# GpSimd applies both layer norms, between its products with C, in a state-space and mixture-of-experts layer

## The reference, cut to what matters

```python
def _layernorm(x, axis=-1, eps=1e-05):
    m = jnp.mean(x, axis=axis, keepdims=True)
    v = jnp.var(x, axis=axis, keepdims=True)
    return (x - m) / jnp.sqrt(v + eps)

h = _L0_tok_ref(x)
h = h + _L0_attn_ref(_layernorm(h, axis=-1), ...)   # y = sum over n of h[n] * C[n], h by a scan
h = h + _L0_ffn_ref(_layernorm(h, axis=-1), ...)
```

## Time and profile before

| | us |
|---|---|
| median of 3 runs | 3821.16 (3820.72 to 3831.04) |
| profiled execution, its own time | 3815.21 |
| span of the trace | 3813.3 |
| busy PE / DVE / ACT / POOL | 3190.2 / 3016.4 / 2879.0 / 2106.1 |
| share of the span PE / DVE / ACT / POOL | 84% / 79% / 75% / 55% |

### The profile page before, as it was taken

How to read it: one execution, slowest core, us unless ns; L and a number is a source line. 1 busy time by engine, 2 the same in 40 slices (tenths; PEclk the granted TensorE clock), 3 DMA queues, 4 the chain that set the end, 5 groups by cost and what they waited for, 6 DMA issues and landing times. The chain is left out here.

```text
span 3813.3 us, 65702 instructions
## 1 busy us (share of the span) xinstructions
PE 3190.2 (84%) x19681; PEld 2528.9 (66%) x19681; DVE 3016.4 (79%) x5267; ACT 2879.0 (75%) x5580; POOL 2106.1 (55%) x780
## 2 busy tenths in 40 slices
PE   5898898988888888888888898898898888566664
PEld 3777776776777677777777777676677667445453
DVE  3888888888888888888888888888888898544442
ACT  4998988888888888888888888888888888121110
POOL 0555555555555555555555555555555556157776
PEclk8999999999999999999999999999999998678887
DMA  2111111111111111111111111111111111157775
GB/s 84 47 47 55 55 43 56 57 57 55 51 53 40 56 57 57 57 57 52 54 57 57 57 55 43 57 57 57 49 56 52 40 52 50 42 135 146 147 151 86
DMA packets 175733, 241.57 MB, mean 63 GB/s; under 512 B 32816, under 2 KB 154128, under 8 KB 175376
## 3 DMA queue, kind: packets, MB, share of 16 engines
q1 hardware_dynamic: 150800, 199.44, 16.3%
q0 software_dynamic: 24576, 37.77, 6.0%
HBM read 176.07 MB, written 61.08 MB: 62 GB/s over the span
## 5 line engine op out<-in xcount | busy, mean ns | idle before, releaser
L345 POOL TENSOR_TENSOR hid<-hid,c_all 128x1536 f32<-128x1536 f32 x512 | 1771.0, 3459 | 1491.6 <-DVEq L563 1489.6
L568 DVE TENSOR_TENSOR_SCAN hid<-decay,hid,psB 128x512 f32<-128x512 f32 x1024 | 1310.7, 1280 | 119.3 <-PE psB L826 12.4
L826 PE MATMUL psB<-ident,dbu_t 128*128 128x128 f32 x6144 | 936.7, 285 | 236.8 <-DVE hid L568 224.0
L363 ACT ACTIVATE dbu_t<-dtu_t,b_t 128x512 f32<-128x512 f32 x1536 | 995.5, 714 | 159.8 <-PE psB L826 158.2
L375 ACT ACTIVATE decay<-dt,a_neg 128x383 f32<-128x383 f32 x2048 | 1085.8, 606 | 0.0
L826 PEld LDWEIGHTS psB<-ident,dbu_t 128*128 128x128 f32 x6144 | 721.8, 145 | 446.6 <-DVE hid L568 325.7
L838 PE MATMUL psY<-ident,hid 128*128 128x128 f32 x6144 | 780.7, 278 | 33.1 <-POOL hid L345 32.3
L838 PEld LDWEIGHTS psY<-ident,hid 128*128 128x128 f32 x6144 | 714.2, 145 | 77.6 <-POOL hid L345 34.4
L568 DVE TENSOR_TENSOR_SCAN hid<-decay,psB 128x512 f32<-128x512 f32 x512 | 624.0, 1219 | 103.4 <-PE psB L826 72.0
L898 PE MATMUL psM<-u,w_dt 128*128 128x384 f32 x1024 | 354.7, 489 | 18.3 <-ACT turned L384 14.7
L898 PEld LDWEIGHTS psM<-u,w_dt 128*128 128x128 f32 x1024 | 184.4, 190 | 127.8 <-ACT turned L384 21.3
(11 more groups left out here) (148 smaller groups left out, 3520.4 us busy)
## 6 DMA issues: line engine op xcount, KB each, us to landing
c_all<-bc_rows_dram SPq DMA_DIRECT2D x128, 768.0 KB, 4.9
out_dram<-h SPq DMA_DIRECT2D x64, 384.0 KB, 3.5
h<-out_dram SPq DMA_DIRECT2D x32, 384.0 KB, 3.4
x_weights_dram<-normed SPq DMA_DIRECT2D x32, 384.0 KB, 2.5
xs<-in_x_dram SPq DMA_DIRECT2D x32, 256.0 KB
e_wg<-in_gate_dram SPq DMA_DIRECT2D x64, 128.0 KB
e_wu<-in_up_dram SPq DMA_DIRECT2D x64, 128.0 KB
e_wd<-in_down_dram SPq DMA_DIRECT2D x64, 128.0 KB
```

What stands on the lines that cost most here:

```text
L345: nc.gpsimd.tensor_tensor(hid[k % 4][:, :, :], hid[k % 4][:, :, :], c_all[:, k, :].unsqueeze(1).to_broadcast([P, CH, L]), ALU.mult).then_i ...
L363: last = nc.scalar.activation(dbu_t[k % 2][:, t, :], dtu_t[q][:, t, :], ACT.Copy, scale=b_t[q][:, t, k:k + 1])
L568: nc.vector.tensor_tensor_scan(h[:, lo:hi], flat(decay[k % 4])[:, lo:hi], psB[:, j, :], h[:, lo - 1:lo] if j else 0.0, ALU.mult, ALU.add). ...
L826: last = nc.tensor.transpose(psB[:, j, i * P:(i + 1) * P], dbu_t[k % 2][:, t, c * P:(c + 1) * P], ident[:, :])
```

## The change

Three pieces. `norm` on DVE keeps the four small operations (as `full_rstd`) and loses the three that apply the norm, together with their waits. POOL gets them, between its products: the second norm ahead of product 4, the first ahead of product 13. POOL's loop of 32 bodies becomes the list of `each`. DVE gets two new waits, for POOL to be done with `h1` before `attended` overwrites it and with `mv[1]` before `second_stats` does.

```diff
-            with pool.Fori(0, NB) as b:
+            def norm(n, j, src, to):
+
+                pool.wait_ge(s_rs[j], n + 1)
+                if j == 1:
+                    pool.wait_ge(s_xst, 16 * (n + 1))
+                pool.sem_inc(s_turn, 1)
+                for s in range(NSEG):
+                    last = nc.gpsimd.tensor_scalar(to[:, s, :], src[:, s, :], mv[j][:, s, 0:1],
+                                                   rstd[j][:, s:s + 1], ALU.subtract, ALU.mult)
+                last.then_inc(s_xn[j], 1)
+
+            def body(b, q, scans, back, late, routed, front, early):
                 for k in range(NS):
-                    times_c(b, k)
+                    if late and k == 4:
+                        norm(b - 2, 1, h2, normed2)
+                    if early and k == 13:
+                        norm(b + 2, 0, h1, normed1)
+                    if scans:
+                        times_c(b, k)
+
+            each(pool, body)
...
-            def norm(n, j, src, to):
+            def full_rstd(n, j):
...
                 nc.vector.tensor_tensor(rstd[j][:, :], t[:, 2, :], y, ALU.mult).then_inc(s_rs[j], 1)
-                dve.wait_ge(s_rs[j], n + 1)
-                if j == 1:
-                    dve.wait_ge(s_xst, 16 * (n + 1))
-                for s in range(NSEG):
-                    last = nc.vector.tensor_scalar(to[:, s, :], src[:, s, :], mv[j][:, s, 0:1],
-                                                   rstd[j][:, s:s + 1], ALU.subtract, ALU.mult)
-                last.then_inc(s_xn[j], 1)
...
                 after(dve, s_h1st, 16 * a)
+                after(dve, s_xn[0], a)
...
             def second_stats(o, b):
+                after(dve, s_xn[1], o)
...
                         if k == 5:
-                            norm(o, 1, h2, normed2)
+                            full_rstd(o, 1)
...
                         if k == 14:
-                            norm(a, 0, h1, normed1)
+                            full_rstd(a, 0)
```

## The result

The changed kernel takes 3863.9 us (median of 4 runs, 3862.47 to 3868.53) beside 3820.94 (4 runs, 3817.2 to 3831.04) for the kernel before: a ratio of 1.0118 with a 95% interval of 1.0102 to 1.0134. It is 43 us slower, not 19 faster. The profiled execution has a span of 3860.3 us, 47 more than before.

What follows compares the result with a forecast made beforehand. No engine was full; waits between PE, DVE and ACT bound the kernel, DVE leading in steps 10 to 5. 20.8 - 2 = 19 us off 3815.2 gave 3796 profiled, so 3802 median; forecast's own range 3795 to 3811, overall 3782 to 3819.

Steps and rivals of the forecast that it cites:

- What leaves DVE: Before the scans of steps 14 and 5: without the norm's three operations the scan begins 0.84 us earlier.
- Step 14: First norm, beside scans in 30 bodies: 0.84 us gained in 17, 0.5 in 13 at loop turns, entry or exit; 20.8 us.
- PE's wait of step 2: PE's 2.14 us wait in step 2 stays about as long, since PE and DVE both move.
- the loop turn: Where the two-body loop turns, PE leads and holds scan 0, so step 14 gains only 0.5 us.
- T: POOL's time for a norm's three operations: 1.5 us, 0.5 each, bounds 1.0 to 10.4; PE waits for products from 3.1.
- rival C: At products 4 and 13, POOL's operation is dear: at 2 us each, 99 us lost, 3920 us; chance 0.08.
- Beside whom it runs: Product 4 overhanging into step 6 could hold L723, DVE's first two-input operation: 0.2 us at T = 1.8, costed at nothing.
- DVE's 3.4 us of waits: DVE's three waits for PE and ACT in step 10, said to grow from 2.5 to 3.4 us.
- the prediction's own signs of being wrong: PE waiting for products, L723 or L725 stretched to over 1 us, or waits in step 10 as long as before.
- rival A: Step 5 pays too, as step 10's waits shrink: 25 us more, 3777 us; chance 0.10.
- the ends: Where the pipeline fills and drains, serial chains take T plus a handover instead of 1.06 us: 4 x 0.5 = 2 us lost.
- Step 5's gain: Second norm, 30 times 0.84 us off DVE, costed at nothing since step 10's waits grow; 25 us if that cover isn't real.

Runs made afterwards that it cites:

- e2: Changed kernel with the second norm applied on DVE again and only the first on POOL; ratio 0.9987 to the kernel before.
- e1: Kernel before with only POOL's program changed, from a loop of 32 one-body turns to the list with a two-body loop; ratio 0.9995 to the kernel before.
- e4: Changed kernel, both norms on POOL, with POOL's program as a loop of one-body turns; ratio 1.0131 to the kernel before.
- e5: Changed kernel with POOL applying the second norm to one of three parts only, the rest left zero; ratio 0.9991 to the kernel before.
- e10: Changed kernel with `route_experts` moved on DVE from step 6 to step 8, nothing left out; ratio 1.0013 to the kernel before.
- e7: Changed kernel with 67 empty instructions at the start of DVE's program; ratio 1.0095 to the kernel before.

## Why the prediction was wrong

**Right.** What leaves DVE: 0.76 us for each norm instead of 0.84, since the gap before the scan is 0.26 behind the refinement and not 0.17. Step 14: the gain is real (13 to 14 shorter by 0.76, shortest sum of e2 lower by 0.63, 16 us in 26 bodies beside 20.8 for 30), and PE follows it. PE's wait of step 2 stays. At the loop turn the gain isn't the smaller 0.5 us of the prediction: the interval from scan 13 to 14 is shorter by 0.76 there too, and e2's turn is no later than before (29.6 us beside 31.0)., from which the prediction read that PE leads at a turn, is of a turn at which PE's granted clock was 0.50 (1671.65 to 1674.47 us of the kernel before); over its twelve loop turns the gap before scan 0 goes from 0.20 to 0.86 us. PE hardly waits for products (at most 0.6 us, once in two sequences; the prediction had such waits begin at T = 3.1). POOL's turned loop costs nothing (e1, e4), and in the waits of the steady stretch DVE doesn't wait for POOL once, so its two new waits cost nothing either. The operation that a product can hold was named correctly.

**The size that was off: POOL's operation.** The prediction took 0.5 us from an AFFINE_SELECT and the product's rate; it takes 1.22, and T is 3.62 us, not 1.5. That is 4.8 ns a column against the product's 2.25. The rows it was taken from are of operations with one step per element and no scalar from a tile; this form has two of each, which may be why, though no run varied it. T stayed inside the bounds (1.0 to 10.4), but what was made of the far side was only rival C at 0.08. The Trainium skill (GPSIMD Engine Reference, Engine selection) calls one-input operations on GpSimd roughly line-rate; here it took 3.4 times DVE's 1.06 us. The prediction's estimate of 2.1 us used that section's figure for two inputs, and was low too.

**The step that failed.** It is in "Beside whom it runs": a hold of L723 would lie "inside DVE's 3.4 us of waits. Nothing." The place was right, and so was the arithmetic: with 0.2 us at T = 1.8 the same line gives 3.62 - 1.6 = 2.0 us at the T measured, and 1.9 came. The price was wrong. The waits it was charged to lie in step 10, and PE needs scan 6 and 7 long before. In step 6 PE has no slack for a late scan (0.35 and 0.74 us of waits at once), so the delay goes on to PE and ACT, the work of PE that DVE awaits in step 10 is late by the same amount, and the waits there stay 0.51, 1.03 and 0.99. Slack of this kind takes up DVE being earlier (part of the second norm's gain, by e5), not DVE being later: a wait for somebody who is himself delayed doesn't shrink. Two of the prediction's own signs of being wrong came with it: L723 (now L736) over 1 us, and waits in step 10 as long as before, which it would have read as rival A. In the bodies 4 to 29 the hold costs 26 x 1.9 = 49 us, and the kernels in which it is gone took 48 (e5) and 40 us (e10) less than the changed kernel.

Rival C named POOL's dear operation, with the break-even at T = 4 to 4.7 from PE's need of the products. Those points held: at 3.62 PE waits hardly at all. The loss came through the other consumer of POOL's time, the shared access to SBUF, whose threshold was at T = 1.6. Its price was not weighed against a T beyond 1.8, though the range of T went to 10.4.

**Not foreseen.** The late instructions: 24 of the 47 us in the profile. Some 15 of them are halts of DVE at the loop turn and in step 1; e7 shows that they follow the program's places. The other 9 are step 9, PE's clock, and this difference may be chance, since kernels with the DVE program of before spread from 5.3 to 12.5 us. The prediction counted DVE's removed instructions as time won and gave no thought to the program's places moving. And the ends: 4 x 0.5 us was taken and 11 came. The bodies there pay the block too, and the norm that costs 3.62 stands in serial chains. Step 5's gain, costed at nothing, would have been 0.43 us a sequence without the block, so rival A was partly right and couldn't show.

**What stays open.** Whether the rest of the gain could be had with a program whose halts all fall into waits. With the four shifts tried on kernels with a norm on POOL the turn had 28.5 to 32.3 us and step 9 10.7 to 25.2, and none won. What makes PE's clock fall in step 9 is open as well. Taking the whole of the norm to POOL in smaller pieces behind several products wasn't tried.

## What to carry to other kernels

Before an operation is laid between others on a second engine, list what the first engine runs beside the work that now ends later, and price a hold at each of them with the largest duration inside your bounds, not the likeliest. Slack seen downstream hides a gain but not a delay: ask at the place of the delay whether the engine's consumer has slack there, and whether the wait you mean to draw on is itself fed by the work you delay. And if a tight loop gets or loses instructions, expect some tenths of a per cent of either sign from where its halts fall; shifting the program by empty instructions tells that from the change itself. Where a step is late in some sequences only, read the granted clock of just that stretch first: over the whole steady stretch it was 0.97 before and after and hid what step 9 shows.

## What the runs showed of the hardware that wasn't expected

- `tensor_scalar` with two scalars from tiles on POOL takes 1.22 us for 128 x 256 float32, and three of them 3.62 us where DVE needs 1.06. That is 4.8 ns a column, whatever fixed part there is included; POOL's two-input product needs 2.25.
- A product of POOL holds not only DVE's operations with two SBUF tiles (2.10 us for 24 columns) but also `tensor_scalar` from SBUF to SBUF with constants (2.08) and with a scalar from a tile (2.10). MAX8, MATCH_REPLACE8, BATCH_NORM_STATS2, scans and additions from PSUM are not held.
- DVE halts about 0.4 us at places a multiple of 128 instructions apart in its program, where no wait hides it, and a turn of its two-body loop costs 1.9 us and, if a halt lies right behind, some 0.8 more. Empty instructions ahead of the loop move the halts.
- Twelve small matmuls of PE take 1.51 us in one sequence, at a granted clock of 1.00, and 2.62 in another, at 0.54. The same place of the pattern gets the lower level in some sequences only, 3 to 17 of 26 by the kernel, and the runs don't show why.
